# GpSimd's B product of the relaid scan issued as two half instructions, each with its own count

## The reference

```python
h = x * rsqrt(mean(x * x) + EPS) * norm_scale
xs, res = split(h @ w_in, 2)                 # 512 channels each
res = silu(res)
xs = silu(causal_depthwise_conv(xs, conv_w, conv_b))
delta, B, C = split(xs @ w_xproj, [16, 32])  # 16 states per channel
delta = softplus(delta @ w_dt + b_dt)
deltaA = exp(delta[..., None] * -exp(A_log))
deltaBx = (delta * xs)[..., None] * B[:, :, None, :]
ys[t] = deltaA[t] * ys[t-1] + deltaBx[t]     # written there as an associative scan
y = einsum('blcn,bln->blc', ys, C)
out = (y + xs * D) * res
x = x + out @ w_out
```

## Time and profile before

| | |
|---|---|
| median of three runs | 1999.08 us |
| the profiled execution | 1994.91 us |
| its span | 1993.0 us |
| granted TensorE clock, mean | 0.892 |
| PE busy | 1553.9 us (78%) |
| DVE busy | 1172.8 us (59%) |
| POOL busy | 1004.7 us (50%) |
| ACT busy | 895.4 us (45%) |

### The profile page before, as it was taken

How to read it: one execution, slowest core, us unless ns; L and a number is a source line. 1 busy time by engine, 2 the same in 40 slices (tenths; PEclk the granted TensorE clock), 3 DMA queues, 4 the chain that set the end, 5 groups by cost and what they waited for, 6 DMA issues and landing times.

```text
span 1993.0 us, 23250 instructions
## 1 busy us (share of the span) xinstructions
PE 1553.9 (78%) x6593; PEld 907.6 (46%) x6594; DVE 1172.8 (59%) x1853; ACT 895.4 (45%) x1666; POOL 1004.7 (50%) x431
## 2 busy tenths in 40 slices
PE   6486877868778688786563999994999999999900
PEld 2121221312213122231022666763999999999800
DVE  3298898888988889888893444422222222222256
ACT  4576676666766657666541343321222222222200
POOL 0598898988988988889881223120000000000075
PEclk9798888989989898797896999996999999999955
DMA  4643426444264442544424301014555555555344
GB/s 126 144 105 98 106 60 143 107 100 103 58 143 107 100 111 54 138 107 101 111 43 144 119 33 42 22 41 162 178 177 180 184 184 184 182 180 177 125 124 129
DMA packets 122137, 235.54 MB, mean 118 GB/s; under 512 B 15584, under 2 KB 53840, under 8 KB 121952
## 3 DMA queue, kind: packets, MB, share of 16 engines
q1 hardware_dynamic: 115936, 218.11, 38.9%
q0 software_dynamic: 6144, 16.79, 2.7%
HBM read 193.69 MB, written 41.16 MB: 118 GB/s over the span
## 4 chain that ended last, share of the span: by engine, by line
PE 46%; POOL 28%; DVE 9%; issue 7%; ACT 5%; DMA 3%; SPq 1%; POOLq 0%; DVEq 0%; ACTq 0%
POOL X L421 15%; PE psH L1469 13%; PE psP L1480 12%; PE psP L1391 6%; PE psH L1400 6%; POOL X L434 5%; DVE psH L973 4%; PE psP L1353 3%; POOL gat L489 2%; POOL ud L406 2%; POOL spe L403 2%; POOL spr L404 2%; POOL ud L409 2%; DVE X L984 1%; PE psA L1342 1%
## 5 line engine op out<-in xcount | busy, mean ns | idle before, releaser
L421 POOL TENSOR_TENSOR X<-rep,B 128x2048 f32<-128x2048 f32 x128 | 576.8, 4525 | 96.6 <-DMA rep<-ud_dram 64.3
L1342 PE MATMUL psA<-X,gsum 128*32 128x512 f32 x1024 | 330.9, 650 | 205.8 <-DVE X L984 188.7
L807 ACT ACTIVATE psH<-rep,A_q 128x512 f32<-128x512 f32 x512 | 350.1, 689 | 170.1 <-DVE X L984 157.1
L489 POOL DMA_INDIRECT gat<-eo_dram,slots x64 | 62.9, 982 | 583.1 <-DVE slots L1216 563.4
L973 DVE TENSOR_TENSOR_SCAN psH<-psH,X 128x512 f32<-128x512 f32 x192 | 233.2, 1220 | 84.3 <-POOL X L421 78.2
L1469 PEld LDWEIGHTS psH<-nTb,ew_s 128*128 128x128 f32 x2272 | 265.9, 193 | 3.6
L1469 PE MATMUL psH<-nTb,ew_s 128*128 128x128 f32 x2272 | 266.1, 276 | 0.0
L973 DVE TENSOR_TENSOR_SCAN psH<-psH,carry,X 128x512 f32<-128x512 f32 x192 | 243.9, 1278 | 33.8 <-POOL X L421 32.5
L1342 PEld LDWEIGHTS psA<-X,gsum 128*32 128x32 f32 x1024 | 45.5, 112 | 478.3 <-DVE X L984 403.1
L897 ACT ACTIVATE hT<-hT 128x512 f32<-128x512 f32 x142 | 89.4, 630 | 384.1 <-DVE hT L1185 384.1
L984 DVE TENSOR_TENSOR X<-psH,C 128x512 f32<-128x512 f32 x384 | 257.9, 672 | 0.0
(11 more groups left out here) (173 smaller groups left out, 1614.5 us busy)
## 6 DMA issues: line engine op xcount, KB each, us to landing
ew_s<-in_L_ffn_ew_dram SPq DMA_DIRECT2D x79, 1024.0 KB, 4.9
rep<-ud_dram SPq DMA_DIRECT2D x128, 512.0 KB, 8.7
ud_dram<-ud SPq DMA_DIRECT2D x32, 512.0 KB, 2.6
xb<-rows_dram SPq DMA_DIRECT2D x71, 128.0 KB, 4.0
eo_dram<-eo SPq DMA_DIRECT2D x71, 128.0 KB, 1.7
B<-bc_dram SPq DMA_DIRECT2D x128, 64.0 KB, 6.3
C<-bc_dram SPq DMA_DIRECT2D x128, 64.0 KB, 7.2
out_dram<-fin SPq DMA_DIRECT2D x8, 512.0 KB, 3.5
```

What stands on the lines that cost most here:

```text
L421: nc.gpsimd.tensor_tensor(X[:, Q % NX], rep[:, g % 2, 1], B4[:, f:f + 1, :].broadcast_to([P, NR, TC]), ALU.mult).then_inc(bx_ready, 1)
L807: nc.scalar.activation(psH[:, r, :], rep[:, g % 2, 0, r, :], ACT.Exp, scale=A_q[:, c, r, f:f + 1]).then_inc(dA_ready, 1)
L1342: ins = nc.tensor.matmul(psA[r * GJ:(r + 1) * GJ, g % 2, :], gsum[:], X[:, Q % NX, r, :], start=False, stop=(f == NF - 1), skip_group_chec ...
```

## The change

The product with B is issued in two halves, row groups 0 and 1 and row groups 2 and 3. Each raises `bx_ready` by 1, so a step now counts 2. The scans of r = 0 wait for the first half and those of r = 2 for the second. The two waits of SyncE on `bx_ready` are doubled to name the same instants. The product with C (L434) stays one instruction.

```diff
@@ input_step (GpSimd) @@
                 if Q >= NX:
                     pool.wait_ge(y_acc, summed(Q - NX))
-                nc.gpsimd.tensor_tensor(X[:, Q % NX], rep[:, g % 2, 1],
-                                        B4[:, f:f + 1, :].broadcast_to([P, NR, TC]),
-                                        ALU.mult).then_inc(bx_ready, 1)
+                for h in range(2):
+                    r = slice(h * (NR // 2), (h + 1) * (NR // 2))
+                    nc.gpsimd.tensor_tensor(X[:, Q % NX, r], rep[:, g % 2, 1, r],
+                                            B4[:, f:f + 1, :].broadcast_to([P, NR // 2, TC]),
+                                            ALU.mult).then_inc(bx_ready, 1)
@@ load_b (SyncE) @@
-                after(sp, bx_ready, (k - 1) * NQ + NQ - NF + f + 1)
+                after(sp, bx_ready, 2 * ((k - 1) * NQ + NQ - NF + f + 1))
@@ load_rep (SyncE) @@
-                after(sp, bx_ready, (g - 2) * NF + NF)
+                after(sp, bx_ready, 2 * ((g - 2) * NF + NF))
@@ scan (VectorE) @@
+                if r % (NR // 2) == 0:
+                    dve.wait_ge(bx_ready, 2 * Q + r // (NR // 2) + 1)
                 if r == 0:
-                    dve.wait_ge(bx_ready, Q + 1)
```

## The result

The changed kernel takes 1989.36 us, the median of six runs (1987.12 to 1995.33), against 2000.65 for the kernel before in the same sessions: 11.3 us less by the medians. The ratio of the runs is 0.995, with a 95% interval of 0.9935 to 0.9966: 10.0 us less (6.8 to 13.0), since two of the six runs, 1992.94 and 1995.33, lie well above the median. The forecast was a gain of 10.7 us and 1988.4.

A forecast was written before the change was run, and what follows sets the result against it. The prediction took GpSimd and VectorE to hold each other up through TensorE and transfers in a cycle repeating each tile. Terms -17.3 and +6.6 gave -10.7 us, 1988.4 against the median 1999.08; range 1981.8 less a microsecond to 1996.

The forecast's parts named there:

- Segment 2: Step 7's product through VectorE's scan and TensorE's chain to GpSimd's step 11: shorter by 2.162 us in tiles 1 to 7.
- cycle of four segments: Waits repeating in each tile between GpSimd, VectorE, TensorE and transfers: steps 4 to 7, 7 to 11, 11 to 0, 0 to 4.
- step 0-4: Segment 4, ending with rep's transfer: splits of steps 0 and 1 cost 0.149 us each, those of 2 and 3 nothing.
- The first term, 17.3: Gain from VectorE starting on step 7's first half (in tile 0 its first scan): eight times 2.162, 17.3 us.
- the wait ahead of step 11: GpSimd's idleness for TensorE's sums: 4.54 us less 2.16 and 0.60 leaves 1.8, covering the splits of steps 7 to 10.
- The second term, 6.6: Cost of splits where GpSimd is the path (steps 4 to 6, 11 to 13, 0, 1): 44 times 0.149, 6.6 us.
- The further wait: VectorE's third scan waits for the second half: costed at 0; at 0.07 in 40 steps it would be 2.8 us.
- ScalarE does not take over: Rival, 8%: in step 7 ScalarE's silu pair holds the scans, the half product buys nothing; +6.6, 2005.7 us.
- my further reason: Behind step 7 TensorE works without a gap to step 11's release, so nothing of ScalarE ends a wait of it there.
- TensorE's clock: Rival, 3%: clock behind step 7 falls from 0.94 to 0.72, +5.8 us in each tile, 2034.
- VectorE's waits on the product: Sign: VectorE's waits on L421 fall from 142.9 us by about 2.2 for each step that waited.
- The tile period from step 4 to step 4: Sign: the period of about 123 us gets 1.0 shorter from an odd tile, 1.4 from an even one.

The follow-up runs named there:

- The two kernels that differ only in the wait: All 128 steps split: with the first scan waiting for both halves 2004.46 us; with the half wait (the changed kernel run again) 1987.79 us.
- all splits together: Changed kernel, all 128 steps split, but the first scan of a step waits for both halves: 2004.46 us, ratio 1.0021.
- The steps under cover: Against the changed kernel, only steps 2, 3, 7 to 10, 14, 15 split, every scan waiting for its whole step: 2001.7 us, ratio 1.0008.
- the second: The changed kernel unchanged, five more rounds: 1987.79 us against 2000.28 for the kernel before, ratio 0.9944.

## Why the prediction was right

**Where the gain comes in: shown.** Segment 2 was the step that carried the forecast, and step 7 to 11 is shorter by 14.5 us in the means of two profiles (212.9 to 198.4). With step 7 whole the kernel is slower than before, +3.7, and with step 7 alone 10.4 of the 17.3 us are missing, so the chain behind its first scan carries the gain, but only if the steps ahead of it come early too. The cycle of four segments holds. Tiles 1 to 6, two profiles of each kernel, against the terms of the sum:

```
us, sum over tiles 1 to 6     step 0-4  step 4-7  step 7-11  step 11-0   all
forecast                        +1.8      +2.7     -13.0       +1.3     -7.2
measured                        +3.8      +2.5     -12.8       +1.0     -5.5
```

Three of the four came out as counted, segment 2 with 2.13 us a tile where 2.162 was taken. Step 0 to 4, which ends with the landing of rep, took 2 us more than its splits. In the four profiles in which every step there is split it is 1.3 to 4.9 longer than before, so the excess is not told apart from scatter. Tile 0 is shorter by 2.2 where 2.16 was expected. In tile 7 step 11 does not wait for TensorE (0 and 0.47 us of idleness before), so the prediction put its gain in the wrong place: step 7 to 11 is 0.3 longer there, and the stretch behind it, which VectorE ends, is 2.1 shorter.

**The first term, 17.3.** The two kernels that differ only in the wait are 16.7 apart. In tile 3 the wait ahead of step 11 fell from 4.54 to 1.83, where 1.8 was worked out. Over tiles 1 to 6 it fell from 5.1 to 2.4 on average, by 2.7, where 2.16 + 0.60 was expected; the single waits of the changed kernel lie between 1.6 and 3.1, because TensorE's chain takes more than 1 us longer in some tiles than in others (below).

**The second term, 6.6, is probably too large.** The constant was right: three split steps take 512.02 - 498.14 = 13.88, 4.627 each, so a split costs 0.154 where 0.149 was taken. The estimate from the Trainium skill (GPSIMD Engine Reference, Performance pitfalls for Q7 kernels), 0.17, is a little high; the page prices read commands, and two of them for a product is my reading. Timed, all splits together cost 4.2 (2.4 to 6.0 by the interval). 2.9 of it is found between steps 4 and 7 of tiles 1 to 7, where 3.1 was expected. That leaves less than the 3.4 that the splits of steps 0, 1 and 11 to 13 had in the sum, and the profiles do not tell which cost less. The kernel with step 7 whole, where the full 6.6 less the 2.2 of the first scan would be +4.4, took +3.7 and has room for all of it. The steps under cover cost 1.3, with 0 in the interval. So the two terms miss by 0.6 and 2.4 us, and that the forecast (-10.7) lies within 0.6 of the first median (-11.3) is in part luck: the second is -12.5.

**The further wait, put at nothing.** In tile 0, where VectorE is behind, its second and third scan start 1.716 us apart before and after, though the third now has the wait for the second half ahead of it. So this wait costs nothing, and not 0.07.

**The rivals.** ScalarE does not take over in the changed kernel: the wait for it in step 7 is 0.40, before 0.55. The prediction's reason, that the pair is released by step 6 and comes early with it, is what the kernel with step 7 alone confirms from the other side, with 10.4 of the 17.3 us gone. But my further reason, that nothing of ScalarE ends a wait of TensorE behind step 7, was only true as long as the pair moved: 2.35 us of such a wait appeared through the residual. TensorE's clock did not fall: in tile 3 it was 0.83 over the last sum and the output projection before, and 0.83 after, and over tiles 1 to 7 of two profiles the two together take 10.4 us on average before and after. What the prediction did not see is that the mix with the 1.2 GHz level was in this chain already; its 0.94 is the average over 19 us.

```profile
503.50:513.40 9.90, 9.80 (x35) 6.93 (x36) 9.35 (x11) 6.63 (x8) 9.90 (x3) 0.83 0.51 104
```

```profile
502.40:512.30 9.90, 9.86 (x35) 7.43 (x36) 9.50 (x11) 6.42 (x8) 9.90 (x6) 0.83 0.53 115
```

The first is the kernel before, the second the changed one, tile 3 (length, busy of PE, PEld, DVE, ACT and POOL, clock, DMA).

**What I had wrong in the signs to look for.** VectorE's waits on the product were to fall by 2.2 us a step; they fell by 2.4 in all (by 6.5 in the mean of two profiles each). The step before ends earlier too, which I had used for step 6 and forgotten here. The tile period from step 4 to step 4 was to be shorter by 1.0 from an odd tile and 1.4 from an even one; it is shorter by 1.3 and 0.8 (tiles 1 to 6, two profiles each), 1.0 on average where 1.2 was expected. The waits for rep ahead of step 4 did not shrink by the 0.3 of steps 2 and 3 in the first profile (6.33 in tile 4 against 5.63 before), which is the excess of step 0 to 4 above.

**Open.** The timed gain (11.3 and 12.5 by the medians, 10.0 and 11.2 by the ratios) is larger than that of the stage in the profiles (8.6), though 8.6 still lies in both intervals (6.8 to 13.0, 8.6 to 14.0). The profiled executions of the changed kernel were the slowest of their runs both times, one of the kernel before lay under all of its own. On average their spans are only 4.0 us apart: the changed kernel's took 1.7 longer ahead of the stage and 2.9 behind it, which nothing in the prediction has. Two profiles of each don't settle whether all of that is scatter. Which splits cost less than 0.15 is open too.

## What to carry over

Where two engines wait for each other in a cycle, handing work over in halves pays where the early start of a step is passed on to whoever ends the next wait (here at one step of 16); find that step in the chain of waits, and pay for the split there and at the steps that must be early for it (here 3 of 16: 1987.0 against 1987.79 and 1989.36 with all split, no slower). An engine's waits need not shrink when all its steps start earlier, so compare periods, not waiting times. One profiled execution can hide a gain of half a per cent: compare segments over several profiles.

## What the runs showed of the hardware

**TensorE's work after an idle time.** In the kernel before TensorE is idle for 3.2 us ahead of the last sum of step 6. Tile 3 of its second profile:

```profile
505.88 1.92 PE L1342 MATMUL psA<-X,gsum 128*32 128x512 f32 x2 [3.22 <-DVE X L984]
507.73 9.18 PE L1353 MATMUL psP<-w_out_s,res 128*128 128x256 f32 x32
```

In the kernel with step 7 alone it is idle for 1.05 to 1.25 us there in tiles 1 to 7, and the same 32 matmuls take 7.17 in all seven. The projection alone, tile 3, in the kernel before, the changed one and the one with step 7 alone:

```profile
505.30:513.40 8.10, 8.10 (x34) 6.74 (x34) 7.55 (x9) 4.85 (x7) 8.10 (x3) 0.88 0.62 126
```

```profile
503.45:512.28 8.83, 8.83 (x34) 7.24 (x34) 8.43 (x11) 5.38 (x8) 8.83 (x5) 0.81 0.60 128
```

```profile
500.70:507.85 7.15, 7.13 (x33) 5.96 (x32) 4.54 (x6) 6.99 (x8) 7.15 (x2) 1.00 0.14 34
```

The granted clock is 1.00, the 2.4 GHz level, in the last and partly 1.2 GHz in the others. In the other nine profiles, tiles 1 to 7, the idle time is 3.1 to 5.7 us, the clock over sum and projection 0.71 to 0.84, and the projection takes 7.7 to 9.4 us. So up to 2.2 us of the chain go with that idle time, and from tile to tile it varies by about as much as the change moves a tile. The transfers beside it differ too (DMA share 0.14 against 0.60 and more), but they have no part in it: length times clock is 7.13, 7.15 and 7.15 in the three rows, and from the first to the last start of the 32 matmuls it is 6.75 to 6.80 us in all 70 projections. The low level can also begin behind the first work and not with it: in the changed kernel's tile 3 the last sum still ran at 1.00 and the fall came in the projection. Closing that gap without holding ScalarE back was not tried.

**GpSimd's pitch and its reported length.** The halves last 2.357 us each in the page, 4.71 a pair, while the starts are 4.627 apart; the next instruction starts before the reported end of the one before. The Trainium skill (Perfetto Trace Analysis, GPSIMD Engine Instruction) advises to time GpSimd by the spacing of starts; the trace agrees, 0.154 by the starts against 0.19 by the lengths (2 times 2.357 less the 4.525 of the page before).
